# Half 0's gather in an expert layer: started by the looked-up last group, and told out one transfer per block, three in four blocks

## What is computed

```python
x = x + 0.5 * _L0_ffn_ref(_layernorm(x, axis=-1), L0_ffn_Wr, L0_ffn_Wg, L0_ffn_Wu, L0_ffn_Wd)
x = x + _L0_attn_ref(_layernorm(x, axis=-1), ...)
x = x + 0.5 * _L0_ffn_ref(_layernorm(x, axis=-1), L0_ffn_Wr, L0_ffn_Wg, L0_ffn_Wu, L0_ffn_Wd)
```

```python
logits = jnp.einsum('th,eh->te', x, Wr)
probs = jax.nn.softmax(logits.astype(jnp.float32), axis=-1)
w, idx = jax.lax.top_k(probs, TOP_K)
w = w / jnp.sum(w, axis=-1, keepdims=True)
combine = jnp.zeros((T, E), x.dtype).at[jnp.arange(T)[:, None], idx].add(w)
gate = jnp.einsum('th,ehi->eti', x, Wg)
up = jnp.einsum('th,ehi->eti', x, Wu)
h = jax.nn.silu(gate) * up
out = jnp.einsum('eti,eih,te->th', h, Wd, combine)
```

## Time and profile before

| | us |
|---|---|
| median of 3 runs | 3611.23 |
| lowest, highest | 3606.42, 3626.48 |
| profiled execution: span from first to last instruction | 3599.5 |
| median of the runs less that span | 11.7 |
| busy: PE, DVE, ACT, POOL | 2897.9, 2374.4, 1820.9, 1539.4 |
| layer 0 ends, layer 1's block loop ends (us from the start) | about 600, 3535 |

### The profile page before, as it was taken

How to read it: one execution, slowest core, us unless ns; L and a number is a source line. 1 busy time by engine, 2 the same in 40 slices (tenths; PEclk the granted TensorE clock), 3 DMA queues, 4 the chain that set the end, 5 groups by cost and what they waited for, 6 DMA issues and landing times.

```text
span 3599.5 us, 84310 instructions
## 1 busy us (share of the span) xinstructions
PE 2897.9 (81%) x28752; PEld 2199.6 (61%) x28752; DVE 2374.4 (66%) x3926; ACT 1820.9 (51%) x3740; POOL 1539.4 (43%) x1420
## 2 busy tenths in 40 slices
PE   5139957788888899999977999999899998279573
PEld 4128846466666657667654667676676676168462
DVE  5214224699999849889945988884888885243135
ACT  1016624566666356666614666663666672046331
POOL 3550050255555416655610555551455553510345
PEclk7559968889899899999978999998999998589785
DMA  9537755466665246556403666642666653467564
GB/s 387 197 123 254 255 163 179 142 183 184 177 184 176 77 139 171 164 162 171 134 3 119 173 172 172 171 134 68 170 172 171 172 160 115 158 206 254 175 205 138
DMA packets 311258, 605.54 MB, mean 168 GB/s; under 512 B 59136, under 2 KB 159616, under 8 KB 310016
## 3 DMA queue, kind: packets, MB, share of 16 engines
q1 hardware_dynamic: 286464, 535.63, 48.9%
q0 software_dynamic: 24576, 67.14, 5.6%
HBM read 446.25 MB, written 155.32 MB: 167 GB/s over the span
## 4 chain that ended last, share of the span: by engine, by line
PE 53%; DVE 19%; issue 10%; another core or an unknown queue 7%; ACT 4%; DMA 4%; POOL 1%; DVEq 1%; SPq 1%; POOLq 0%; ACTq 0%
PE bank L63 15%; PE bank L568 7%; PE bank L1327 4%; DVE tmp L1275 3%; PE bank L1197 3%; PE bank L1393 3%; DVE xbc L1251 3%; DMA rc_in<-decay_t 3%; PE bank L581 2%; PE bank L559 2%; PE bank L1391 2%; PE cs_sn L581 2%; PE bank L1367 2%; DVE rot L1275 2%
## 5 line engine op out<-in xcount | busy, mean ns | idle before, releaser
L63 PE MATMUL bank<-xh,wb 128*128 128x512 f32 x2048 | 685.4, 416 | 73.1 <-ACT btr L1342 43.2
L644 DVE TENSOR_TENSOR hh<-sg,bank 128x96 f32<-128x96 f32 x384 | 97.5, 254 | 596.4 <-ACT sg L619 372.6
L63 PEld LDWEIGHTS bank<-xh,wb 128*128 128x128 f32 x2048 | 373.3, 192 | 190.4 <-ACT btr L1342 63.9
L1206 ACT ACTIVATE xbc<-bank,norm_w 128x512 f32<-128x512 f32 x512 | 350.7, 685 | 240.8 <-PE bank L63 234.1
L1295 POOL TENSOR_TENSOR sq<-cst,rho 128x512 f32<-128x512 f32 x128 | 133.5, 1043 | 742.8 <-DVE xbc L1251 411.3
L1283 POOL TENSOR_TENSOR rot<-rot,tmp 128x512 f32<-128x512 f32 x256 | 341.8, 1335 | 238.3 <-DVE tmp L1275 238.3
L568 PE MATMUL bank<-wgu,xgT 128*128 (+1 forms) x1536 | 343.7, 350 | 107.6 <-issue 68.2
L63 PE MATMUL bank<-xl,wb 128*128 128x512 f32 x1024 | 408.5, 399 | 0.0
L1284 POOL TENSOR_TENSOR rot<-rot,tmp 128x512 f32<-128x512 f32 x256 | 358.7, 1401 | 0.0
L568 PEld LDWEIGHTS bank<-wgu,xgT 128*128 128x128 f32 x1536 | 261.0, 204 | 118.5 <-issue 118.1
L1275 DVE SCALAR_TENSOR_TENSOR rot<-xbc,bias,cs_sn 128x1024 f32<-128x1024 f32 x256 | 325.4, 1271 | 8.4 <-DVE xbc L1251 6.8
(11 more groups left out here) (277 smaller groups left out, 6084.7 us busy)
## 6 DMA issues: line engine op xcount, KB each, us to landing
wb<-watt_dram SPq DMA_DIRECT2D x96, 1024.0 KB, 7.7
rr_bc<-rr_dram SPq DMA_DIRECT2D x128, 512.0 KB
yd<-ys SPq DMA_DIRECT2D x96, 512.0 KB
wd<-w_down SPq DMA_DIRECT2D x384, 96.0 KB
watt_dram<-wb SPq DMA_DIRECT2D x32, 1024.0 KB, 5.4
dt_bc<-row_dram SPq DMA_DIRECT2D x256, 128.0 KB
al_bc<-row_dram SPq DMA_DIRECT2D x256, 128.0 KB, 3.2
xd<-xg SPq DMA_DIRECT2D x12, 2048.0 KB, 23.7
```

The source lines that it names most:

```text
L63: ins = e.matmul(dst, a, m, start=start and c == 0, stop=stop and c == n - 1, skip_group_check=not (start and stop))
L1206: e.activation(xbc[j % 4][:, i, :], of(i)[:, :], ACT.Copy, scale=norm_w[:, i:i + 1])
```

## The change

The gather of half 0 is started and paced in another way, alike in both layers:

- It waits for the looked-up number of groups in layer 0 too.
- Each of its 64 transfers also waits for e_hh, which DVE raises once per block. Transfer i waits for `paced(i)` = 110 + 4i // 3 blocks, at most 191. That is 110, 111, 112, 114, 115, 116, 118 and so on: three transfers, one per block, then a block without one.
- DVE combines transfer i ten blocks later, at `combined(i)` = `paced(i)` + 10, from block 120 on. Again 54 are inside the loop and 10 behind it. The tiles' transposes and adds on PE and DVE move along.
- In layer 0 SP also fills yd's blocks 96 to 127 with zeros (4 MB), and waits for it before the first load of the block loop.

```diff
@@ build
+        a_yz = arr("a_yz")
@@ gather_pool
             if t == 0:
-                if g == 0:
-                    e.wait_ge(e_land.sem, e_land.at(NRB // 4))
-                else:
-                    e.wait_ge(e_land.sem, e.value_load(need[0:1, NE // 4 + h:NE // 4 + h + 1], min_val=e_land.at((LB + HEAD + NE) // 4),
-                                                       max_val=e_land.at(2 * LB // 4)))
-                    e.nop(nofuse=True)
+                done = g // NH2 * LB
+                e.wait_ge(e_land.sem, e.value_load(need[0:1, NE // 4 + h:NE // 4 + h + 1], min_val=e_land.at((done + HEAD + NE) // 4),
+                                                   max_val=e_land.at((done + LB) // 4)))
+                e.nop(nofuse=True)
...
             for k in range(TOPK):
                 c = (h * RT + t) * TOPK + k
+                if h == 0:
+                    e.wait_ge(e_hh.sem, e_hh.at(g // NH2 * LB + min(paced(t * TOPK + k), LB - 1)))
@@ ahead of blocks_pe
+        START, LATE = 110, 10
-        tile_end = lambda t: NRB + LATE + TOPK * (t + 1)
+        paced = lambda i: START + 4 * i // 3
+        combined = lambda i: paced(i) + LATE
+        in_blocks = [t for t in range(RT) if combined(t * TOPK + TOPK - 1) + 5 < LB]
@@ blocks_pe
-                for t in range(RT - 2):
-                    if n == tile_end(t) + 3:
+                for t in in_blocks:
+                    if n == combined(t * TOPK + TOPK - 1) + 3:
                         token_pe(e, NH2 * c, t)
-            for t in range(RT - 2, RT):
+            for t in range(len(in_blocks), RT):
                 token_pe(e, NH2 * c, t)
@@ blocks_dve
-                i = n - NRB - LATE
-                if 0 <= i and n < LB:
-                    combine_dve(e, NH2 * c, i // TOPK, i % TOPK)
-                for t in range(RT - 2):
-                    if n == tile_end(t) + 5:
+                for i in range(RT * TOPK):
+                    if n == combined(i) and n < LB:
+                        combine_dve(e, NH2 * c, i // TOPK, i % TOPK)
+                for t in in_blocks:
+                    if n == combined(t * TOPK + TOPK - 1) + 5:
                         token_dve(e, NH2 * c, t)
...
@@ blocks_sp
             e.wait_ge(a_zf[1].sem, a_zf[1].at(4))
+            e.wait_ge(a_yz.sem, a_yz.at(1))
@@ ffn_sp
                 zero_fill_sp(e, 1, 1)
+                rows = yd[(HEAD + NE) * P:NRB * P, :].rearrange("(p b) d -> p (b d)", p=P)
+                e.dma_start(rows.rearrange("p (b d) -> p b d", d=D), xg[2][:, 0:1, :].to_broadcast([P, NRB - HEAD - NE, D])).then_inc(a_yz.sem, 16)
```

More of the change, by code:

```diff
@@ L658, in blocks_dve @@
                     match_dve(e, NH2 * c + 1, 1, n - 4)
-                i = n - NRB - LATE
-                if 0 <= i and n < LB:
-                    combine_dve(e, NH2 * c, i // TOPK, i % TOPK)
-                for t in range(RT - 2):
-                    if n == tile_end(t) + 5:
-                        token_dve(e, NH2 * c, t)
-            for i in range(LB - NRB - LATE, RT * TOPK):
-                combine_dve(e, NH2 * c, i // TOPK, i % TOPK)
-                if i % TOPK == TOPK - 1:
-                    token_dve(e, NH2 * c, i // TOPK)
-        LATE = 10
+                for i in range(RT * TOPK):
[3 more added lines that the diff above has]
+                    if n == combined(t * TOPK + TOPK - 1) + 5:
+                        token_dve(e, NH2 * c, t)
+            for t in range(len(in_blocks), RT):
+                for k in range(TOPK):
+                    if combined(t * TOPK + k) >= LB:
+                        combine_dve(e, NH2 * c, t, k)
+                token_dve(e, NH2 * c, t)
         by_four = lambda a, m: a[4 * P * m:4 * P * (m + 1), :].rearrange("(p b) d -> p (b d)", b=4)
```

## The result

| | before | after |
|---|---|---|
| median (lowest to highest), us | 3608.82 (3604.99 to 3626.48), 4 runs | 3492.72 (3488.53 to 3497.24), 4 runs |
| profiled execution, span in us | 3599.5 | 3489.5 |
| block 110's hh to block 190's, layer 0 | 184.5 | 126.0 |
| the same, layer 1 | 210.7 | 124.6 |
| block 190's hh in layer 1 to the end | 66.4 | 95.9 |

The change is faster: ratio 0.9673, 95% interval 0.9654 to 0.9691. That holds for the conditions under which the kernel before takes some 3610 us. In a second group of runs the same kernel before took 3352 to 3355 us, and there the change is not faster; this is told with the experiments, in two groups.

What follows compares the result with a forecast made beforehand. It took late hand-offs out of PE during back-to-back gathers as the bound. Layer 0 -42.2, layer 1's loop -68.5 and its tail +31.3 gave -79.4 us: span 3520.1, median 3532 us, 8-in-10 range 3483 to 3614.

Steps and rivals of the forecast that it cites:

- p: Block loops of both layers: block time lost per gather let go between blocks, taken as 0.45 us.
- The straight line: Block loop: loss against burst length, through bursts of 8 and 40 gathers; 1.7 us for three back to back.
- nearly free: Rival, block loops: a paced gather costs up to 0.2 us, taken at 0.1; 3487 us, chance 0.17.
- the case of equal cost: Rival: about 1.07 us per gather, so the loops gain only what the tail loses; 3611 us, chance 0.21.
- the bound by bandwidth: Block loop: block plus 0.75 gather needs 1.43 us of all DMA engines against 1.42, so about 0.02 us per gather.
- Each costs the same: Rival, block loops: pacing leaves a gather's price at about 1.07 us, no gain; 3611 us, chance 0.21.
- The slower rival: Block loops: gathers spread over all 80 blocks leave no calm stretch, PE's clock stays low; 3649 us, chance 0.10.
- Late landing: Rival, layer 0: data lands after block 110, first gathers follow back to back; +12 us at most, 3544, chance 0.03.
- The tail: End of layer 1: half 1's gathers stand behind half 0's last three, which wait for 191 blocks; +31.3 us.
- Layer 0's tail: After layer 0's block loop: ten combine steps remain as before; costed at 0, at most 2 us.
- The fill: Before the block loop: SP's 4 MB more of zeros, hidden by the second routing; taken as 0, up to 5 us.
- The page's rule: DMA queues: engines go round-robin between software- and hardware-generated descriptors, so gathers would cost only their share; the free case.

Runs made afterwards that it cites:

- e2: The changed kernel with half 0's gathers let go in runs of three back to back, same mean rate: 3511.58 us.
- f3: The kernel before, unedited, run once more with a profile: 3616.78 us, span 3615.0.
- e4: The changed kernel with one gather per block and none left out, in layer 1 half 1's paced behind half 0's: 3493.04 us.
- e8: The changed kernel with yd's fill sent late and, in layer 1 only, one gather per block with half 1's paced behind: 3341.03 us.
- g1: As e8, but layer 0's gathers spaced by a POOL fill, waiting only for the first block: 3345.52 us, ratio 0.9978 to the kernel before.
- e7: The changed kernel with half 0's gathers let go in runs of five back to back, same mean rate: 3368.51 us.

## Why the prediction was right or wrong

**The sum's form held.** It was 128p - 137.0 on the span. By its own rule for p (the stretch less 113.4, over 64) p was 0.20 and 0.17, which gives -113.3, and the span moved by -110.0 us. What bounds the dips at this level (hand-offs out of PE that come late while gathers follow each other), which terms there are and their signs were right.

**The step that failed is the size of p.** I took 0.45, "nearer the latter, because 1.418 is nearly back to back". The rows showed 0.21 and 0.18, so the loops gained 58.5 and 86.1 us where the text has 42.2 and 68.5. Two things were wrong in that step. The straight line through runs of 8 and 40 doesn't hold below 8 (it gave 1.7 us for three, e2 0.94): three truly back to back cost 0.31 to 0.33 each (e2), not 0.6, so even the upper end was too high. And "they come 1.418 us apart" took the blocks as even, where late blocks and those that catch up let up to three gathers go at 1.46 us or less, and as many stand further apart. What keeps the price low is, as far as the runs show, that no run is longer than three: as a gather waits for a block's hh, a fourth can't follow before the blocks have caught up.

**The likeliest case was the wrong neighbour.** The rival "nearly free" (p up to 0.2; 3487 us) is what happened: 3492.7 us, outside the forecast's own 3500 to 3593 and inside the range of 3483 to 3614. It had 0.17 of the chance, so the direction was foreseen and the size was not: of the 39 us between 3532 and 3492.7, 34 are p. The upper end of that range, 3614, is p = 1.09, so it held only part of the case of equal cost, which ran to 1.2. What should have spoken louder for it is that the bound by bandwidth sufficed and that the two bursts were both long; the only row against it, the late hand-off of the earlier trace rows, was real (1.65 us again), but the blocks behind it recovered. It was also misread as standing behind the very first gather: in before as in after the SiLU behind one gather was on time, and the late one stands behind the third.

**Each costs the same, slower:** both fell at the first level. The slower rival rested on the clock staying low over all 80 blocks; it was 1.00. **Late landing:** the prediction had the wait for 110 blocks as the later one in layer 0. It was landing, by 0.8 us: the first gather was at 408.50, near enough for no block to be lost.

**The tail** was +31.3 and measured +29.5; 85.5 us from block 190's hh to the last issue, 87.3 forecast. Half 1's 64 stood behind the wait for 191 blocks, as the order shows. This term is most of what makes the change lose at the second level: there it is the same size and the loops have little to give.

**Layer 0's tail** was put at 0 to 2: its last add ended at 544.95, 10.1 us after block 190's hh against 9.6, +0.5.

**The fill** was put at 0, at most 5. The measured +5.2 before block 0 is just over that bound, the kernel before shows 4.8 by itself between two executions (f3), and the fill's own cost stays open.

**The distance between span and median** was 11.7 us. Each run of after has 1.8 us around its span; the rest was that the profiled execution of the kernel before was below its median. In after the distance is 3.2 us, so this made the forecast 8.5 us too high.

**The page's rule.** In the paced stretch the DMA share is 0.90, and the calm share plus the gathers' own gives 0.77 x 113.4 / 126.0 + 61 x 0.45 / 126.0 = 0.91. The page "DMA: Bandwidth & Descriptors" of the Trainium skill, section "SWDGE vs HWDGE vs iDMA", has the engines go round-robin between the queues. By that rule gathers would cost only their share. For spaced gathers the trace agrees on the share, but a gather cost 0.2 us where the prediction's working gave 0.02. For eight in a run at the first level it disagrees (1.03 us at a share of 0.63); what the trace shows there is late hand-offs out of PE.

## What to carry to other kernels

Count a transfer's cost on the rest of the kernel by how closely it follows others, not by how many there are: some 64 gathers between blocks cost 66 us in runs of eight, 20 in runs of three and 13 let go by the blocks one at a time, with the same bytes over the same blocks. A wait that paces one queue by the work it disturbs was cheap here, but everything behind it on that queue moves too: let it end early enough, or let what follows it into the loop (e4, e8, g1), before counting the gain. And time a change at more than one occasion with the kernel before beside it: this one is 3.3% faster at one level of the device and 0.6% slower at another. To see which level a profile is of, compare the end of an engine's product with the start of the step that waits for it, beside a run of indirect transfers.

## What the runs showed of the hardware

- **The price jumps.** 0.33 us per gather in runs of three (1.4 us apart), 1.03 in runs of eight (1.26 us apart). With the long runs the granted clock falls from 1.00 to 0.84. Where between three and eight it turns wasn't found, since e7 fell in the second group.
- **Late hand-offs are made up for.** Behind three gathers, SiLU waits 1.65 us for PE, and the next block's follows 0.67 us later. The hand-off from ACT to DVE stays at 0.03 us in these stretches, in the burst too. Only in runs is there no block to catch up in. This reading is argued from the timeline and from the prices, not shown by a run of its own.
- **Two levels.** Unedited, the kernel before takes 3605 to 3626 us or 3343 to 3364 us, by the occasion. The change takes 3493 or 3371. At the first level up to 44 of 384 SiLUs start late behind PE's product, by up to 10 us, beside indirect transfers; at the second none does. The calm 80 periods are equal (113.7 and 113.6 us); blocks 0 to 30, beside half 1's scatter, take 116.1 or 83.5 us. What switches the late hand-offs on isn't known. At both levels those blocks take far more than 30 free periods (42.5 us), so a scatter paced by the blocks is the next thing to try; it wasn't tried here.
